# Moving VectorE's gated product of the attention output ahead of the aggregated residual statistics

## The reference, cut to what matters

```python
sim = einsum('bgid,bgjd->bgij', quad_q, quad_k) / g + t5_rel_bias(rel_table)
attn = where(causal_mask, 0.0, square(relu(sim)))
quad_out = einsum('bgij,bgje->bgie', attn, vg)
lin_kv = pad(cumsum(einsum('bgnd,bgne->bgde', lin_k, vg) / g))[:, :-1]
lin_out = einsum('bgde,bgnd->bgne', lin_kv, lin_q)
out = gate * (quad_out + lin_out)            # the gated product
return out @ Wout + bout + x
# and around each block:
x = x + layernorm(block(layernorm(x)))       # "residual" = what the block returns
```

## Time and profile before

| | us |
|---|---|
| median of 3 runs | 613.88 (611.25 to 617.87) |
| the profiled execution | 615.71 |
| its span, first to last instruction | 613.9 |
| TensorE busy, of the span | 498.2 (81%) |
| VectorE busy | 473.7 (77%) |
| ScalarE busy | 282.5 (46%) |
| GpSimd busy | 326.5 (53%) |
| mean granted TensorE clock | 0.936 |

### The profile page before, as it was taken

One profiled execution on the slowest core, in us unless ns is written; L12 is line 12 of the kernel. 1 busy time (PEld: TensorE's weight loads), 2 busy tenths in 40 slices (PEclk: granted clock), 3 DMA queues, 4 the chain that ended last, 5 costly groups with the idle time before them and its releaser, 6 DMA issues.

```text
span 613.9 us, 10624 instructions
## 1 busy us (share of the span) xinstructions
PE 498.2 (81%) x2943; PEld 406.1 (66%) x2959; DVE 473.7 (77%) x1726; ACT 282.5 (46%) x608; POOL 326.5 (53%) x384
## 2 busy tenths in 40 slices
PE   1999499999877877778578797689778978889991
PEld 0565277877756766666456585578777868778881
DVE  2456868999998989968485577688778888689974
ACT  2444374655554444114334464464445455545540
POOL 5547236564778787755570578367575132323432
PEclk9999799999999899777799998899889999999996
DMA  7600069994000010124455885122121000000111
GB/s 201 196 1 2 6 183 286 286 287 133 18 11 26 14 32 17 34 80 134 130 176 167 259 266 161 41 63 69 43 61 44 2 1 2 1 2 18 36 35 52
DMA packets 74154, 54.85 MB, mean 89 GB/s; under 512 B 5614, under 2 KB 69614, under 8 KB 74095
## 3 DMA queue, kind: packets, MB, share of 16 engines
q1 hardware_dynamic: 68976, 41.58, 22.8%
q0 software_dynamic: 5120, 12.59, 6.9%
HBM read 19.70 MB, written 34.45 MB: 88 GB/s over the span
## 4 chain that ended last, share of the span: by engine, by line
PE 34%; DVE 27%; issue 15%; POOL 14%; ACT 3%; DMA 3%; SPq 1%; DVEq 0%; POOLq 0%; ACTq 0%
POOL shared_buf L545 5%; PE ps L1758 4%; PE ps L1759 3%; PE ps L1760 3%; POOL z_rows L532 3%; POOL rstds L517 3%; PE ps L1832 2%; DMA g_rows<-slot_g 2%; DVE X L1109 2%; PE ps L1831 2%; PE ps L2132 2%; DVE rstats_t L1147 2%; PE ps L1769 2%; PE ps L2137 2%; POOL tails L642 1%
## 5 line engine op out<-in xcount | busy, mean ns | idle before, releaser
L545 POOL DMA_INDIRECT shared_buf<-g_rows,back x64 | 62.0, 968 | 40.6 <-DMA g_rows<-slot_g 16.6
L532 POOL DMA_INDIRECT z_rows<-Z,dest x64 | 64.5, 1008 | 22.1 <-issue 16.6
L517 POOL TENSOR_TENSOR rstds<-vars_t,mhalf 128x4 f32<-128x4 f32 (+1 forms) x24 | 31.2, 1299 | 74.9 <-DVE vars_t L1096 38.1
L752 ACT ACTIVATE Z<-X,shift,rstds 128x128 f32<-128x128 f32 x128 | 53.3, 482 | 18.7 <-DVE shift L1073 12.5
L1758 PE MATMUL ps<-w_hi,ZT_hi 128*128 (+1 forms) x110 | 48.8, 444 | 10.6 <-DVE ZT_lo L1554 9.1
L918 ACT ACTIVATE half_tanh<-ps 128x256 f32<-128x256 f32 x78 | 29.5, 384 | 46.0 <-PE ps L1760 44.8
L1562 DVE SCALAR_TENSOR_TENSOR slot_g<-half_tanh,ps 128x256 f32<-128x256 f32 x78 | 31.6, 416 | 22.4 <-ACT half_tanh L918 13.0
L1759 PE MATMUL ps<-w_lo,ZT_hi 128*128 (+1 forms) x110 | 43.1, 392 | 0.0
L1760 PE MATMUL ps<-w_hi,ZT_lo 128*128 (+1 forms) x110 | 42.8, 389 | 0.0
L522 POOL TENSOR_TENSOR res_rstd<-rvar,mhalf 128x4 f32<-128x4 f32 x24 | 24.7, 1031 | 28.0 <-DVE rvar L1164 28.0
L1929 PE MATMUL ps<-dtx,Edec 128*128 128x64 f32 x256 | 35.6, 285 | 0.9 <-DVE tails L1510 0.9
(11 more groups left out here) (307 smaller groups left out, 1588.3 us busy)
## 6 DMA issues: line engine op xcount, KB each, us to landing
z_rows<-zero SPq DMA_DIRECT2D x34, 512.0 KB, 6.7
g_rows<-slot_g SPq DMA_DIRECT2D x38, 256.0 KB, 2.9
slot_zs<-z_rows SPq DMA_DIRECT2D x78, 64.0 KB, 2.0
X<-in_x SPq DMA_DIRECT2D x4, 512.0 KB, 6.3
RES<-in_W1T SPq DMA_DIRECT2D x4, 512.0 KB, 5.5
out<-X SPq DMA_DIRECT2D x8, 256.0 KB, 2.3
z_rows<-Z,dest POOLq DMA_INDIRECT x64, 2.3
shared_buf<-g_rows,back POOLq DMA_INDIRECT x64, 3.0
```

Source lines behind the costliest of these rows:

```text
L517: pool.tensor_tensor(rstds[:, 0:k], vars_t[:, 0:k], mhalf[:, 0:k], ALU.pow).then_inc(zpow_made, 1)
L532: pool.indirect_dma_start(z_rows[group(i)], bass.IndirectOffsetOnAxis(ap=dest[:, i, k, c:c + 1], axis=0), Zr[i % 4][:, c], None).then_inc( ...
L545: pool.indirect_dma_start(got[:, c, k], None, g_rows[group(i)], bass.IndirectOffsetOnAxis(ap=back[:, i, k, c:c + 1], axis=0))\
L752: act.activation(dst[:, c], X[:, i, c], ACT.Identity, bias=shift[:, c:c + 1], scale=rstds[:, k, c:c + 1]).then_inc(z_made, 1)
```

## The change

In stages 0 to 4 the statistics of the expert residual are cut in two: `rbn_stats(2, i+3)` stays in front of the gated product, `rbn_aggr(2, i+3)` goes between its halves. In stages 1 to 7 the whole `rstats(3, i-1)` goes behind both halves. No instruction is added or removed, on any engine.

```diff
                 if moe:
                     residB(i + 3, 4)
-                    rstats(2, i + 3)
-                if i > 0:
-                    rstats(3, i - 1)
+                    rbn_stats(2, i + 3)
                 if last:
                     for m in range(EARLY_D):
                         gatedD(0, m, 0)
                 for half in range(2):
                     dve.wait_ge(o_made, i * 2 + half + 1)
                     dve.wait_ge(cact_made, i * 5 + 2 + half)
                     dve.wait_ge(cout_made, i)
                     dve.tensor_tensor(og[:, half], bank(6 + half), gt[par][:, half], ALU.mult).then_inc(og_made, 1)
+                    if half == 0 and moe:
+                        rbn_aggr(2, i + 3)
+                if i > 0:
+                    rstats(3, i - 1)
                 if last:
                     lo(3, 1, ZT_lo[1][:], ZT_hi[1][:])
```

## The result

The changed kernel took 595.16 us (median of 4 runs, 591.54 to 597.68), against 612.57 for the kernel before (4 runs, 610.55 to 617.87): a ratio of 0.970, with an interval from 0.962 to 0.978. (The ratio of a comparison leaves out runs more than 1.5% above the fastest of their kernel, and it isn't that of the medians, which is 0.972 here; a time with a number of runs beside it is the median of all of them.) The forecast was 600.8 us, 13.1 us less than the 613.88 us of the three runs before that were known then.

The account below looks back on a forecast made before the run. TensorE's scores waited 10.9 us, in 5 cases, for the gated product, queued behind VectorE's wait for GpSimd. Gains of 12.36 + 1.75 less 0.99 give 13.12 us, taking the median 613.88 to 600.8 us; range 597.8 to 606.5.

Parts of the forecast that it names:

- The wait moved off the product, stages 1 to 4: Scores start without a gap at 12.92 us after `lo`; `lo` to `lo` becomes 16.64 us in these stages.
- Rival 4: TensorE's scores really wait for something else than the product; only stage 7's loss is left, 614.9 us; chance 0.04.
- The clock: Scores in stages 1 to 3 run at granted clock 1.00 instead of 0.50, worth 1.53 us of each stage.
- Rival 2: The clock stays down: scores to `lo` remain 5.25 us in stages 1 to 3, giving 605.4 us; chance 0.07.
- Every stage without the gap of 2.5 us shows 1.00: Argument against a clock that stays down: without that TensorE gap ahead of the scores, the granted clock is always full.
- Half 0's place: Stages 1 to 3: half 0 takes the expert aggregate's slot at about 427.75 without waiting; the aggregate follows 0.60 us later.
- The combines beside `res_rstd`: Stages 1 to 3: two VectorE combines run before GpSimd's bias addition, taking 0.87 us, not 1.89.
- rival 1: Combines run into GpSimd's bias addition; if both take 1.89 us, `lo` is 0.7 us later per stage: 602.8 us; chance 0.10.
- rival 1's second case: Second combine held until GpSimd's bias addition ends: 1.6 us later in each of three stages, 605.5 us.
- Stage 0: Only the expert part moves: half 0 and the aggregate swap places, half 1 ends where it did, nothing gained.
- Stage 7: A loss: statistics between half 1 and `lo` put `lo` 0.99 us later, all charged.
- The sum: 12.36 us for stages 1 to 3, plus 1.75 for stage 4, less 0.99 for stage 7: 13.12 us.

Follow-up runs that it names:

- experiment 4: Kernel before, plus three idle TensorE matmuls in the gap ahead of the scores in stages 1 to 3: 605.68 us (10 runs), ratio 0.990.
- experiment 1: No edit: changed kernel again, 598.09 us (6 runs), ratio 0.975 to the kernel before; kernel before against itself, 611.88 us (10 runs), ratio 1.001.
- experiment 5: Forty transposes into an unused bank while TensorE waits for the first input: 600.46 us (4 runs) in the changed kernel, 612.69 (10 runs) in the one before.
- Experiment 2: Changed kernel with one part alone: attention statistics behind the product, 600.80 us, ratio 0.982; or half 0 ahead of the expert aggregate, 607.65 us, ratio 0.990.
- 7: Changed kernel, but expert aggregate in front of both halves and stage 7 in its old order: 595.32 us (6 runs), ratio 0.977; changed kernel again: 597.41 us.

## Why the prediction was wrong, and where it was right

- *The wait moved off the product, stages 1 to 4.* Right, to 0.05 us a stage: 16.60 for 16.64. Rival 4 fell.
- *The clock.* Right: 1.00 instead of 0.50, worth 1.53 us a stage by forecast, 1.6 by experiment 4. Rival 2 fell. "Every stage without the gap of 2.5 us shows 1.00" was too strong, though: in two later profiles stage 0 lost 1.6 us behind a gap of 1.88 (experiment 1, and the changed kernel with the filler of experiment 5). The Trainium skill's TensorE: Matmul & The Clock Gate (HAM oscillation) bears on this with its advice to restructure a loop so that TensorE stays warm; the filled gap agrees.
- *Half 0's place.* The forecast counted it as needed only to let half 1 through. Experiment 2 shows that it isn't needed at all: what pays is the attention part.
- *The combines beside `res_rstd`.* Right: 0.87 us for two in stages 1 to 3, so rival 1 fell there. In stage 0 the second combine was held for 1.7 us, but behind cover. The size of rival 1's second case was worked out wrongly: a combine held until L + 16.55 puts `lo` at L + 17.84, 1.2 us late and not 1.6, so 604.4 us and not 605.5, and the upper end of the range 605.4.
- *Stage 0.* "Half 1 ends where it did" was wrong by 0.26 us: an idle time of 0.29 us in front of half 1 came with the swap, in every profile that has it, and is gone without it (experiments 2 and 7).
- *Stage 7.* The term was mis-sized: 0.99 us in the sum, 2.03 measured (1.02 up to `lo`, as forecast, and 1.01 behind it). I followed `lo` and what stands behind it on VectorE, but not GpSimd's queue: I had written that a moved statistic delays `res_rstd` and its bias, but only for the stages with gathers.
- *The sum.* 13.12 by forecast, 12.0 in the profiles; stages 0 and 7 are the difference of 1.1 us (0.27 + 1.01, less 0.2 that stages 1 to 4 gave more).
- *The step that failed* is the one from the sum to the time, "the forecast less the 3 us by which a median of such runs can lie low". I took the first 401 us of the program as the same in both kernels, and read the scatter from three runs. The start alone covers 10 us from profile to profile, and single runs of the kernel before lie from 603.6 to 623.1. The forecast missed by 5.6 us. Of these 1.2 are its base (613.88 for a mean of 612.7), and 2.4 that the first four runs of the changed kernel lay below the mean of all its 16 (597.6): luck. The sum for stage C, 1.1 us too large, works the other way. The 3.1 us that are left are those that stay open above: a start faster by chance, or for where the program lies. With the repeats the time would be 597.4 to 598.1 us, 2.7 to 3.4 us below the forecast and at the range's lower end.

## What to carry to other kernels

Where an in-order engine waits inside a group of work, ask which of the instructions behind the wait another engine stands for, and put just these in front: here two products of 1.28 us, held for 1.15 us of waiting and 1.4 us of statistics, cost TensorE 2.5 us and then, mostly, its clock. When a step is moved, follow its result into the queue of the engine that takes it as well: what stands there behind it moves too, and can land on someone. And before a range is written down, look for a part of the profile whose speed is left to chance, since it sets how far two medians can differ.

## What the hardware showed that I had not expected

- TensorE, busy without a gap from 12.6 us on, stayed at the low level until 54 us in one execution and until 28 in another, in kernels with the same start; the first convolution, which waits for it, came between 59.0 and 70.6 us in 13 profiles (two with the filler). The granted clock of the records read 1.00 in a slow part at the very start (the matmul pair of 1.92 us at 26.46) and 0.50 to 0.52 in later ones. The Trainium skill's TensorE: Matmul & The Clock Gate (What's actually happening) says that the number of cold matmuls at a kernel's start differs from run to run, and puts their cost below 1% of a typical span; in this kernel the difference between two executions reached 1.9% (11.6 of 600 us).
- Behind a gap of 2.5 to 2.9 us the scores lost the high level in 8 of 9 cases (stages 1 to 3 of three profiles in the old order), behind one of 1.88 us in 2 of 7 profiles (stage 0).
- GpSimd's addition of 1.25 to 1.45 us with two operands in SBUF holds a VectorE instruction with two operands in SBUF until it ends: a combine of 0.47 us took 2.14, a product of `x_add` 1.36 us instead of 0.35. The Trainium skill's GPSIMD Engine Reference (Specifications) names the shared interfaces; GpSimd's power, with 4 columns, held none of them in stages 1 to 3.
- In stage 0 the held combine started at 408.08, 0.6 us ahead of the addition, beside GpSimd's power (407.65 to 408.69), and was held all the same. What held it that early stays open.
